# A wavelet convolution kernel with a similarity filter: norms kept as strips, six loads per unit instead of eleven, one store per band, another order of the residual's matmuls, and raw statistics one unit later

## The chip, the cores and the metric

The kernel runs on one core of a Trainium2 chip. The metric is device time in microseconds (us) of one launch. The kernel before took 2227.2, 2228.85 and 2239.03 us in three runs, median 2228.85 us.

## The reference

The input `x` is a batch of 8 images, 32 channels, 128 x 128, float32. Two layers follow one another, each of them on a group norm with 32 groups (here one channel each) and added to its input:

```
x = x + L0(gn(x))     # three Haar levels; at each a 5x5 convolution, 128 -> 128 channels, on the
                      # four stacked half-size bands; then the inverse transform, plus a bias
x = x + L1(gn(x))     # below, with the 25 patches (shifted images) of a pixel
    dot    = einsum('bchw,bckhw->bkhw', x, patches)
    sim    = dot / maximum(|x| * |patch|, 1e-8)
    weight = (sim + 1) * 0.5 * spatial_weight[k]
    out    = einsum('bckhw,bkhw->bchw', patches, weight)
```

## The kernel before

**Stages.** The program loops over images. In one pass it does the convolutions of image i and, in the same stretch, the similarity layer of image i - 1 (b in the code). The first pass has convolutions alone, the last the similarity layer alone, so there are eight image stages with a similarity layer. An image at half size has four quadrants of 32 channels, which fill the 128 partitions.

**Units.** The similarity layer of an image is cut into 8 units: four bands of rows, two halves each. For every unit (h or u in the code) ScalarE and VectorE make normalised vectors (`st_hl`, high and low fp16 part), values (`st_v`, the same) and norms (`st_n`). TensorE adds the squares over channels (`norm_piece`, two pieces per unit, into `stat_ps`), ScalarE keeps them and takes roots (`norms`), VectorE refines (`units_open`, `units_refine`, `units_close`, `value_lows`, `unit_lows`), ScalarE counts pixels whose norm is so small that the 1e-8 decides (`count_own`); only where this count is not zero does a guard path run. Each unit has 4 overlapping column groups (strips) of 10 columns; `st_hl` and `st_v` are kept as strips (4 x 18 x 10 = 720 elements), `st_n` as an image (18 x 34 = 612).

**The way through DRAM.** The layout must turn from "quadrant and channel in partitions" to "channel in partitions, quadrants along the row". `save_half` on SP's queue writes a unit's `st_hl`, `st_v` and `st_n` to DRAM in five transfers, `load_unit` reads them back in eleven: two for the keys, four for the queries, one for the values, four for the norm strips of 72 pieces with 10 elements each. SP's order within an image stage is save 0, load 0, save 1, load 1, save 2, and then for u = 0 to 7: the store of a finished band of rows (u = 2, 4, 6), save u + 3, load u + 2. A load of unit u waits until the save of the same unit has landed, and (from u = 2) until TensorE has used up unit u - 2, whose buffer it takes. Units have two buffers in `unit_mem`.

**Unit by unit.** After the level-2 and level-1 convolutions TensorE runs the 8 units. Each has 8 Gram products (`gram`), 30 matmuls of the level-0 convolution, the norm pieces of unit u + 3, the transposed values (`key_values`), the residual image (`residual`, 16 matmuls into 4 column groups) and four filter groups (`filter_group`), all woven together by the list `HOOKS`. VectorE turns every Gram product into weights (`weights`) and does its part of the convolution and the preparation of unit u + 3 between these. `unit_here` is TensorE's wait for a unit's loads.

**The other queue.** POOL's queue carries the raw image, in 8 chunks, once for statistics and once for use, through a ring of four slots; the small level-2 and level-1 images `d_z2` and `d_z1`; and `up`, their upsampled copies. ScalarE may write again over the buffer `z1` only when the save of `d_z1` has landed.

**Lines.** L381, L383 and L384 save a unit. L399 loads keys, L402 queries, L404 values, L409 norm strips. L416 stores a band. L454 and L483 are POOL's raw and `up` loads. L1339 is the Gram product, L1297 the norm piece, L1364 the residual, L1375 the filter.

Of the kernel before, what the change touches and what calls it, by code (L numbers as in the profile page):

```python
# [21 lines left out]
F32 = mybir.dt.float32  # L22
# [6 lines left out]
P = 128  # L29
C = 32  # L30
# [48 lines left out]
SAVES, LOADS = 80, 176  # L79
# [4 lines left out]
PAD_EDGE = P * (SH + SW - 1)  # L84
# [71 lines left out]
def build(nc, x, w0, w1, w2, bias, spatial, square, gather, tapmask, unpair, out):  # L156
    ctx = ExitStack()
    with ctx:
# [27 lines left out]
        st_n = sb("st_n", [P, 2, UN], F32)  # L186
# [59 lines left out]
        d_n = dram("d_n", [B, 2 * BANDS, Q, UN], F32)  # L246
# [113 lines left out]
        def _(sp):  # L360
# [16 lines left out]
            def save_half(b, h):  # L377
# [6 lines left out]
                sp.dma_start(d_n[b, h], st_n[0:P:C, h % 2, :]).then_inc(half_saved[h % 2], 16)  # L384

            def load_unit(b, u):
# [19 lines left out]
                norms = d_n[b, u].rearrange("(a q) (h w) -> a (q h) w", a=1, w=SW)  # L406
# [31 lines left out]
            sp.wait_ge(stored, START + 4 * 64 * B)  # L438
# [3 lines left out]
        def _(pool):  # L442
# [42 lines left out]
            def iteration(i, nxt, conv, ls):  # L485
                if conv:
# [10 lines left out]
                    raw_for_stats(i + 1, nxt, range(SLOTS, CHUNKS))  # L497
# [26 lines left out]
        def _(act):  # L524
# [44 lines left out]
            def result(b, u):  # L569
# [5 lines left out]
                if half == 0:  # L575
                    act.wait_ge(stored, START + 64 * (4 * b + r))
# [46 lines left out]
            def norms(b, h, p):  # L623
# [8 lines left out]
                copy(st_n[:, h % 2, p * PIECE:(p + 1) * PIECE], stat_ps[:, 0:PIECE]).then_inc(n2_kept, 1)  # L632
                if p == 1:
                    act.wait_ge(n2_kept, START + 16 * b + 2 * h + 2)
                    act.wait_ge(unit_low, START + 8 * b + h)
                    copy(st_b[:, :], st_a[:, :], func=ACT.Square).then_inc(root_squared, 1)
                    copy(in_strips(st_v[:, 0, h % 2, :]), strips(st_x2[:, h % 2, :, :].rearrange("p h w -> p (h w)"))).then_inc(v_high, 1)

            def count_own(b, h):
# [3 lines left out]
                nc.scalar.activation(st_hl[:, 1, h % 2, 0:UN], st_n[:, h % 2, :], ACT.Sign, bias=edge[:, :], scale=-1.0,  # L643
# [11 lines left out]
            def iteration(i, conv, ls):  # L655
# [45 lines left out]
                for j in range(CONV_TILES):  # L701
                    if conv and j == 2:
                        root(gn1, gn1_var, gn1_root, i + 1)
# [52 lines left out]
        def _(dve):  # L756
# [190 lines left out]
            def units_open(b, h):  # L947
# [7 lines left out]
                ch.link(dve, V.scalar_tensor_tensor(out=st_b[:, :], in0=st_b[:, :], scalar=-0.5, in1=st_n[:, h % 2, :],  # L955
                                                    op0=ALU.mult, op1=ALU.mult))

            def units_refine(h):
                sq = st_n[:, h % 2, :]
# [583 lines left out]
```

## Time and profile before

| | us |
|---|---|
| median of three runs | 2228.85 |
| the profiled execution | 2231.01 |
| its span in the trace | 2229.3 |
| TensorE matmul busy | 1737.3 |
| VectorE busy | 1363.9 |
| ScalarE busy | 742.9 |
| POOL busy | 430.6 |

### The profile page before, as it was taken

The page shows a single profiled execution, that of the slowest core. Times are in us where ns is not written, and L with a number is a line of the kernel's source. Part 1 is how long each engine was busy: PE and PEld are TensorE (multiplying, and loading weights), DVE is VectorE, ACT ScalarE, POOL GpSimd, SP SyncE. Part 2 cuts the span into 40 slices and gives each one's busy share as a digit, 9 for nine tenths or more (in the row PEclk, how much of TensorE's full clock was granted, in tenths as well). Part 3 has the DMA queues.
Part 4 walks back from the last instruction along what each step waited for, and adds up shares of the span by engine and source line. Part 5 has one row for each costly group of instructions (what it writes and reads, how often), then busy time and mean ns, then how long its engine had stood idle before and what let it go on. Part 6 is the DMA issues. An engine that isn't in the chain of part 4 may idle for free.

```text
span 2229.3 us, 53057 instructions
## 1 busy us (share of the span) xinstructions
PE 1737.3 (78%) x19007; PEld 988.9 (44%) x19007; DVE 1363.9 (61%) x1995; ACT 742.9 (33%) x1318; POOL 430.6 (19%) x760
## 2 busy tenths in 40 slices
PE   5776887978878787878778787878779787876576
PEld 3542344545444444535345344545345444443354
DVE  6427756756677456856577456755578465865453
ACT  2320243423333243423333243423333252423341
POOL 1343322012311123012310123012300224010000
PEclk7888897889989898989989898999989898987577
DMA  5243337552666337562656447552754447571555
GB/s 164 75 106 95 85 104 174 151 137 78 187 155 159 94 104 191 153 140 78 179 156 151 97 114 196 152 139 79 176 149 128 117 105 201 127 174 38 141 145 127
DMA packets 128073, 296.57 MB, mean 133 GB/s; under 512 B 44532, under 2 KB 77300, under 8 KB 127220
## 3 DMA queue, kind: packets, MB, share of 16 engines
q1 hardware_dynamic: 90864, 190.39, 33.5%
q0 software_dynamic: 36864, 101.47, 17.6%
q8 instruction: 230, 3.77, 0.8%
q14 instruction: 115, 0.94, 0.1%
HBM read 221.92 MB, written 69.83 MB: 131 GB/s over the span
## 4 chain that ended last, share of the span: by engine, by line
PE 41%; DMA 17%; DVE 15%; SPq 13%; issue 10%; ACT 2%; DVEq 1%; POOL 1%; ACTq 0%; POOLq 0%
PE conv L1274 11%; DMA unit_mem<-d_n 8%; DMA d_n<-st_n 8%; PE conv L1248 6%; PE gram L1339 5%; PE out_ps L1364 5%; PE out_ps L1375 3%; SPq L409 3%; PE conv L1233 3%; PE stat_ps L1297 3%; SPq L383 3%; SPq L402 2%; SPq L381 2%; PE vals_ps L1322 2%; PE conv L1484 2%
## 5 line engine op out<-in xcount | busy, mean ns | idle before, releaser
L1012 DVE SCALAR_TENSOR_TENSOR wgt<-gram,tapw 124x512 f32<-124x512 f32 x512 | 350.1, 685 | 476.9 <-PE gram L1339 441.2
L1274 PE MATMUL conv<-thl,wconv 128*128 128x496 f16 (+2 forms) x1920 | 535.5, 407 | 20.0 <-DVE xa L892 10.7
L454 POOL DMA_DIRECT2D ring<-in_x x576 | 334.1, 585 | 666.5 <-ACT xa L526 345.0
L1339 PE MATMUL gram<-unit_mem 128*60 128x128 f16 x4096 | 250.6, 247 | 210.1 <-DMA unit_mem<-d_n 137.9
L1339 PEld LDWEIGHTS gram<-unit_mem 128*60 128x60 f16 x4096 | 152.3, 113 | 420.0 <-issue 419.5
L1274 PEld LDWEIGHTS conv<-thl,wconv 128*128 128x128 f16 x1920 | 167.3, 103 | 215.3 <-issue 62.1
L1248 PE MATMUL conv<-thl,wconv 128*128 128x480 f16 (+7 forms) x1200 | 256.9, 368 | 0.0
L483 POOL DMA_DIRECT2D up<-d_z x128 | 68.5, 537 | 813.1 <-DVE xa L943 755.4
L1297 PE MATMUL stat_ps<-st_sq,sq_c 128*128 128x306 f32 x256 | 117.9, 549 | 125.5 <-DVE flag L993 40.4
L1375 PE MATMUL out_ps<-wgt,vals 124*32 124x128 f32 x4096 | 204.8, 296 | 0.8 <-DVE wgt L1012 0.4
L526 ACT ACTIVATE vals<-vals_ps 124x512 f32<-124x512 f32 x128 | 76.2, 596 | 341.3 <-PE vals_ps L1322 337.6
L526 ACT ACTIVATE thl<-tw 128x1024 f16<-128x1024 f32 x64 | 67.6, 1057 | 339.8 <-DVE tw L828 186.4
L1248 PEld LDWEIGHTS conv<-thl,wconv 128*128 128x128 f16 x1200 | 116.1, 98 | 123.4 <-issue 8.8
L1364 PE MATMUL out_ps<-x,sq_c 128*32 128x128 f32 x2048 | 169.0, 289 | 0.0
L1364 PEld LDWEIGHTS out_ps<-x,sq_c 128*32 128x32 f32 x2048 | 147.9, 115 | 19.9 <-issue 16.2
L526 ACT ACTIVATE st_a<-stat_ps,tiny 128x306 f32<-128x306 f32 x128 | 65.7, 514 | 218.4 <-DMA d_n<-st_n 112.3
L1375 PEld LDWEIGHTS out_ps<-wgt,vals 124*32 124x32 f32 x4096 | 124.3, 115 | 29.3 <-issue 6.4
L526 ACT ACTIVATE ostage<-out_ps,live 128x256 f32<-128x256 f32 x128 | 55.0, 486 | 205.2 <-PE out_ps L1375 205.2
L1297 PEld LDWEIGHTS stat_ps<-st_sq,sq_c 128*128 128x128 f32 x256 | 47.6, 223 | 151.6 <-issue 92.3
L955 DVE SCALAR_TENSOR_TENSOR st_b<-st_b,st_n 128x612 f32<-128x612 f32 x64 | 50.5, 789 | 104.5 <-ACT st_b L526 104.0
L1233 PE MATMUL conv<-xa,gat_c 128*128 128x512 f32 x128 | 79.0, 773 | 35.4 <-issue 19.1
L1322 PE MATMUL vals_ps<-unpair_c,unit_mem 64*60 64x32 f16 x4096 | 89.5, 183 | 1.7 <-issue 1.6
(137 smaller groups left out, 2110.8 us busy)
## 6 DMA issues: line engine op xcount, KB each, us to landing
unit_mem<-d_hl SPq DMA_DIRECT2D x128, 360.0 KB
unit_mem<-d_hl SPq DMA_DIRECT2D x256, 180.0 KB
ring<-in_x POOLq DMA_DIRECT2D x288, 128.0 KB, 3.4
ring<-in_x POOLq DMA_DIRECT2D x288, 127.0 KB, 3.7
d_hl<-st_hl SPq DMA_DIRECT2D x128, 180.0 KB
d_v<-st_v SPq DMA_DIRECT2D x128, 180.0 KB
unit_mem<-d_v SPq DMA_DIRECT2D x64, 360.0 KB
up<-d_z POOLq DMA_DIRECT2D x160, 128.0 KB, 4.9
```

Source lines behind the costliest of these rows:

```text
L454: pool.dma_start(dst, src).then_inc(raw_in[slot], 16)
L483: pool.dma_start(up[C * q:C * q + C, :].rearrange("c (b n) -> c b n", b=2), src).then_inc(up_in, 16)
L526: return nc.scalar.activation(dst, src, func, bias=bias, scale=scale)
L1012: V.scalar_tensor_tensor(out=dst, in0=g, scalar=SIM_SCALE ** 2, in1=tapw[:, :].unsqueeze(1).to_broadcast([KN, 2, 2 * QN]), op0=ALU.add, op ...
L1233: last = mm(dst, gat_c[:, q, :], src[:, 2 * r0 + q // 2:2 * r1:2, q % 2:2 * side:2], start=(q == 0), stop=(q == Q - 1))
L1248: last = mm(dst[:, a0 - r0:a1 - r0, b0:b1], wconv[:, level - 1, w, t, :], src[:, a0 + dy:a1 + dy, b0 + dx:b1 + dx], start=(n == 0), stop=( ...
L1274: last = mm(dst[:, :, b0:b1], wconv0[:, w, 2 * (p % ROWS4) + s, dx + 2, :], thl[:, p % 2, d, s, :, b0 + dx:b1 + dx] if p % ROWS4 != 1 else ...
L1297: mm(stat_ps[:, 0:PIECE], same_quadrant, st_sq[:, p * PIECE:(p + 1) * PIECE], start=True, stop=True)\
L1322: last = mm(vals_ps[row:row + KQ, C * n:C * n + C], values[s][0:2 * C, q, e, TH * KW * g:TH * KW * g + KQ], unpair_c[:, :], start=True, st ...
L1339: last = mm(bank[row:row + KQ, col:col + QN], key[:, q, e_at, TH * KW * g:TH * KW * g + KQ], tile[:, :, TH * g + 1:TH * g + 1 + TH, 1:1 + ...
L1364: last = mm(o[C * g:C * g + C, q, :].rearrange("p (h w) -> p h w", h=TH), ident[:, C * q:C * q + C], x1[:, row:row + TH, UW * half:UW * (h ...
L1375: last = mm(o[C * g:C * g + C, :, :, TW * e:TW * e + TW], vals[:, (e * BANDS + g) * 2 + c, :], wgt[:, e % 2, g, c * QN:(c + 1) * QN], star ...
```

## The change

Six edits.

- The norms are written as strips by VectorE (`st_s`, two buffers), and saved as strips, so that a unit's norm strips load as two contiguous rows. `st_n` has one buffer. The wait for the save before last moves from the copy of the norms to ScalarE's copy of the values and VectorE's write of the strips. Counting and the guard path follow the new layout and scale.
- Keys load in one transfer and queries in two. The source of each begins with a dimension of 2 and step 0.
- A band is stored in one transfer, whose DRAM side begins with the dimension of four groups.
- The residual's matmuls run over quadrants outside and column groups inside.
- VectorE's raw statistics of the next image move from ahead of and inside unit 0 to units 0 and 1, the group norm's steps after them by one unit.
- On POOL's queue the raw loads 4 to 7 for statistics come after the save of `d_z1` and its first `up` load, and `up` load 1 ahead of the raw loads for use.

The core of the diff (without constants of the count, and the lines that only pass a parameter on):

```diff
-SAVES, LOADS = 80, 176
+SAVES, LOADS, BAND_STORES = 80, 96, 16
@@ tensors
-        st_n = sb("st_n", [P, 2, UN], F32)
+        st_n, st_s = sb("st_n", [P, UN], F32), sb("st_s", [P, 2, FN], F32)
-        d_n = dram("d_n", [B, 2 * BANDS, Q, UN], F32)
+        d_n = dram("d_n", [B, 2 * BANDS, GROUPS, Q, SN], F32)
@@ SP: save_half
-                sp.dma_start(d_n[b, h], st_n[0:P:C, h % 2, :]).then_inc(half_saved[h % 2], 16)
+                sp.dma_start(d_n[b, h].rearrange("e q n -> q e n"), st_s[0:P:C, h % 2, :].rearrange("p (e n) -> p e n", e=GROUPS)).then_inc(half_saved[h % 2], 16)
@@ SP: load_unit
-                for j in range(2):
-                    sp.dma_start(keys[s][2 * C * j:2 * C * (j + 1)].rearrange("c q e n -> c (q e n)"),
-                                 d_hl[b, u].rearrange("l c q n -> (l c) (q n)")).then_inc(unit_in[s], 16)
-                for j, hl in enumerate((0, 0, 1, 1)):
-                    sp.dma_start(queries[s][C * j:C * j + C].rearrange("c q e n -> c (q e n)"),
-                                 d_hl[b, u, hl].rearrange("c q n -> c (q n)")).then_inc(unit_in[s], 16)
+                sp.dma_start(keys[s].rearrange("p q e n -> p (q e n)"),
+                             d_hl[b, u].rearrange("(a l) c q n -> a (l c) (q n)", a=1).to_broadcast([2, 2 * C, Q * FN])).then_inc(unit_in[s], 16)
+                for hl in range(2):
+                    sp.dma_start(queries[s][2 * C * hl:2 * C * (hl + 1)].rearrange("p q e n -> p (q e n)"),
+                                 d_hl[b, u, hl:hl + 1].rearrange("l c q n -> l c (q n)").to_broadcast([2, C, Q * FN])).then_inc(unit_in[s], 16)
...
-                for e in range(GROUPS):
-                    row = 64 + C * (e // 2)
-                    sp.dma_start(norm_strips[s][row:row + 1, e % 2].rearrange("a (n w) -> a n w", w=KW),
-                                 norms[:, :, TW * e:TW * e + KW]).then_inc(unit_in[s], 16)
+                for a in range(2):
+                    row = 64 + C * a
+                    sp.dma_start(norm_strips[s][row:row + 1].rearrange("p e n -> p (e n)"),
+                                 d_n[b, u, 2 * a:2 * a + 2].rearrange("(p e) q n -> p (e q n)", p=1)).then_inc(unit_in[s], 16)
@@ SP: store_band
-                for g in range(BANDS):
-                    row = 2 * (BH * r + TH * g)
-                    sp.dma_start(out[b, :, row:row + 2 * TH, :].rearrange("c h w -> c (h w)"),
-                                 ostage[C * g:C * g + C].rearrange("c h w -> c (h w)")).then_inc(stored, 16)
+                rows = out[b, :, 2 * BH * r:2 * BH * (r + 1), :].rearrange("c (g h) w -> g c (h w)", g=BANDS)
+                sp.dma_start(rows, ostage[:, :, :].rearrange("p h w -> p (h w)")).then_inc(stored, 16)
@@ POOL: iteration
-                    raw_for_stats(i + 1, nxt, range(SLOTS, CHUNKS))
                     pool.wait_ge(z1_done, 2 * i + 2)
...
                     load_up(i, 0)
+                    raw_for_stats(i + 1, nxt, range(SLOTS, CHUNKS))
+                    load_up(i, 1)
                     raw_for_split(i + 1, nxt, range(SLOTS))
-                    load_up(i, 1)
@@ ACT: norms
-                    act.wait_ge(half_saved[h % 2], START + SAVES * (4 * b + h // 2))
...
                     copy(st_b[:, :], st_a[:, :], func=ACT.Square).then_inc(root_squared, 1)
+                    act.wait_ge(half_saved[h % 2], START + SAVES * (4 * b + h // 2))
@@ DVE: units_refine
-                prep_chain.link(dve, V.scalar_tensor_tensor(out=sq, in0=sq, scalar=EPS_SIM ** -0.5, in1=st_a[:, :],
-                                                            op0=ALU.mult, op1=ALU.mult))
+                dve.wait_ge(half_saved[h % 2], START + SAVES * (4 * b + h // 2))
+                prep_chain.link(dve, V.tensor_tensor(in_strips(st_s[:, h % 2, :]), strips(st_n[:, :]), strips(st_a[:, :]), ALU.mult))
@@ DVE: iteration
-                    raw_stats(i + 1, 0)
-                    raw_stats(i + 1, 1)
                     level1_out(i, 0)
...
-                            if k < 4 and j == 0:
-                                raw_stats(i + 1, SLOTS + k)
+                            if k < 4 and j < 2:
+                                raw_stats(i + 1, SLOTS * j + k)
@@ PE: residual
-                for g in range(BANDS):
-                    row = BH * r + TH * g
-                    for q in range(Q):
+                for q in range(Q):
+                    for g in range(BANDS):
+                        row = BH * r + TH * g
```

SP's queue, first image stage: the end of save 0 and the whole of load 0, with the sizes of each transfer's destination. Before:

```order
L383 DMA d_v<-st_v 4x32x720 x2
L384 ISA
L384 DMA d_n<-st_n 4x612
L388 ISA
L396 ISA
L399 DMA unit_mem<-d_hl 64x2880 x2
L402 DMA unit_mem<-d_hl 32x2880 x4
L404 DMA unit_mem<-d_v 64x2880
L409 DMA unit_mem<-d_n 1x72x10
L409 ISA
```

The last transfer comes four times in all. The same place in the changed kernel:

```order
L383 DMA d_v<-st_v 4x32x720 x2
L384 ISA
L384 DMA d_n<-st_s 4x4x180
L388 ISA
L396 ISA
L398 DMA unit_mem<-d_hl 128x1x2880
L401 DMA unit_mem<-d_hl 64x1x2880 x2
L403 DMA unit_mem<-d_v 64x2880
L407 DMA unit_mem<-d_n 1x1440
L407 ISA
```

Eleven load instructions have become six, with the same bytes. Keys fill 128 partitions at once and queries 64 each; their sources, which the rows don't show, have the sizes 2 x 64 x 2880 and 2 x 32 x 2880.

POOL's queue in the pass of the first image, around the save of the level-1 image (`d_z<-sd`); `ring` is the raw image. Before:

```order
L454 DMA ring<-in_x 32x8x128
L454 DMA ring<-in_x 32x8x127
L499 DMA d_z<-sd 128x1024
L483 DMA up<-d_z 32x2x512 x4
L454 DMA ring<-in_x 32x8x128
L454 DMA ring<-in_x 32x8x127
```

And in the changed kernel:

```order
L485 DMA d_z<-z 128x256
L491 DMA up<-d_z 32x4x256 x4
L494 DMA d_z<-sd 128x1024
L479 DMA up<-d_z 32x2x512 x4
L450 DMA ring<-in_x 32x8x128
L450 DMA ring<-in_x 32x8x127
```

The 16 raw loads that stood ahead of the level-1 image's save now stand behind it and its first `up` load.

## Rows read from the trace of the kernel before

**Rows 1.** The page: span, engine totals, chain that ended last.
```profile
span 2229.3 us, 53057 instructions
...
PE 41%; DMA 17%; DVE 15%; SPq 13%; issue 10%; ACT 2%; DVEq 1%; POOL 1%; ACTq 0%; POOLq 0%
PE conv L1274 11%; DMA unit_mem<-d_n 8%; DMA d_n<-st_n 8%; PE conv L1248 6%; PE gram L1339 5%; PE out_ps L1364 5%; PE out_ps L1375 3%; SPq L409 3%; PE conv L1233 3%; PE stat_ps L1297 3%; SPq L383 3%; SPq L402 2%; SPq L381 2%; PE vals_ps L1322 2%; PE conv L1484 2%
```

**Rows 2.** SP's queue, third of eight image stages: start us, length us, issue.
```profile
807.11 1.50 SPq L381 DMA_DIRECT2D d_hl<-st_hl  x2
...
810.26 0.57 SPq L384 DMA_DIRECT2D d_n<-st_n  x1
818.24 1.23 SPq L399 DMA_DIRECT2D unit_mem<-d_hl  x2
...
821.59 0.47 SPq L404 DMA_DIRECT2D unit_mem<-d_v  x1
822.16 4.08 SPq L409 DMA_DIRECT2D unit_mem<-d_n  x4
...
841.99 1.22 SPq L399 DMA_DIRECT2D unit_mem<-d_hl  x2
...
970.35 1.16 SPq L399 DMA_DIRECT2D unit_mem<-d_hl  x2
```

**Rows 3.** TensorE, same image, units 6 and 7: start us, length us, idle before.
```profile
984.87 0.63 PE L1339 MATMUL gram<-unit_mem 128*60 128x128 f16 x8 [13.46 <-DMA unit_mem<-d_n]
...
1003.31 0.47 PE L1339 MATMUL gram<-unit_mem 128*60 128x128 f16 x8 [0.26 <-issue]
...
1019.80 0.64 PE L1375 MATMUL out_ps<-wgt,vals 124*32 124x128 f32 x16
```

**Rows 4.** Stretches of 1 us: engines busy, PEclk, DMA share, GB/s.
```profile
810.00:811.00 1.00, 1.00 (x6) 0.49 (x5) 0.97 (x2) 1.00 (x3) 0.00 (x0) 1.00 0.27 98
...
816.00:817.00 1.00, 1.00 (x5) 0.53 (x6) 0.00 (x0) 0.00 (x0) 0.00 (x0) 1.00 0.26 94
...
820.00:821.00 1.00, 1.00 (x7) 0.59 (x5) 0.00 (x0) 0.02 (x1) 0.00 (x0) 1.00 0.97 276
...
825.00:826.00 1.00, 1.00 (x6) 0.47 (x5) 0.97 (x3) 0.85 (x3) 0.00 (x0) 1.00 1.07 225
...
847.00:848.00 1.00, 1.00 (x28) 1.00 (x27) 0.60 (x1) 0.00 (x0) 0.00 (x0) 1.00 0.97 368
```

**Rows 5.** The view of the DMAs: queues' totals, transfers by size.
```profile
q0 software_dynamic: 36864, 101.47, 17.6%
q8 instruction: 230, 3.77, 0.8%
...
unit_mem<-d_hl SPq DMA_DIRECT2D x128, 360.0 KB
unit_mem<-d_hl SPq DMA_DIRECT2D x256, 180.0 KB
...
d_hl<-st_hl SPq DMA_DIRECT2D x128, 180.0 KB
...
unit_mem<-d_v SPq DMA_DIRECT2D x64, 360.0 KB
...
out<-ostage SPq DMA_DIRECT2D x128, 128.0 KB, 3.2
```

**Rows 6.** SP's queue, last image stage: first and last unit load.
```profile
2067.87 1.23 SPq L399 DMA_DIRECT2D unit_mem<-d_hl  x2
...
2197.33 1.49 SPq L399 DMA_DIRECT2D unit_mem<-d_hl  x2
```

**Rows 7.** TensorE: unit 1's second norm piece, residual and filter of unit 2.
```profile
871.10 1.39 PE L1297 MATMUL stat_ps<-st_sq,sq_c 128*128 128x306 f32 x2 [4.95 <-ACT st_n L526]
...
899.30 2.13 PE L1364 MATMUL out_ps<-x,sq_c 128*32 128x128 f32 x29
...
903.89 0.65 PE L1375 MATMUL out_ps<-wgt,vals 124*32 124x128 f32 x16
```

More of the change, by code:

```diff
@@ L628, in norms @@
                     act.wait_ge(unit_vec, START + 8 * b + h)
-                    act.wait_ge(half_saved[h % 2], START + SAVES * (4 * b + h // 2))
                 copy(st_a[:, p * PIECE:(p + 1) * PIECE], stat_ps[:, 0:PIECE], func=ACT.Abs_reciprocal_sqrt,
                      bias=tiny[:, :])
-                copy(st_n[:, h % 2, p * PIECE:(p + 1) * PIECE], stat_ps[:, 0:PIECE]).then_inc(n2_kept, 1)
+                copy(st_n[:, p * PIECE:(p + 1) * PIECE], stat_ps[:, 0:PIECE]).then_inc(n2_kept, 1)
                 if p == 1:
@@ L701, in iteration @@
                 for j in range(CONV_TILES):
-                    if conv and j == 2:
+                    if conv and j == 3:
                         root(gn1, gn1_var, gn1_root, i + 1)
@@ L954, in units_open, with units_refine @@
                 dve.wait_ge(root_squared, 8 * b + h + 1)
-                ch.link(dve, V.scalar_tensor_tensor(out=st_b[:, :], in0=st_b[:, :], scalar=-0.5, in1=st_n[:, h % 2, :],
+                ch.link(dve, V.scalar_tensor_tensor(out=st_b[:, :], in0=st_b[:, :], scalar=-0.5, in1=st_n[:, :],
                                                     op0=ALU.mult, op1=ALU.mult))
-            def units_refine(h):
-                sq = st_n[:, h % 2, :]
+            def units_refine(b, h):
                 prep_chain.link(dve, V.scalar_tensor_tensor(out=st_a[:, :], in0=st_b[:, :], scalar=1.5, in1=st_a[:, :],
                                                             op0=ALU.add, op1=ALU.mult))
-                prep_chain.link(dve, V.scalar_tensor_tensor(out=sq, in0=sq, scalar=EPS_SIM ** -0.5, in1=st_a[:, :],
-                                                            op0=ALU.mult, op1=ALU.mult))
+                dve.wait_ge(half_saved[h % 2], START + SAVES * (4 * b + h // 2))
+                prep_chain.link(dve, V.tensor_tensor(in_strips(st_s[:, h % 2, :]), strips(st_n[:, :]), strips(st_a[:, :]), ALU.mult))
             def image_of(h):
@@ L992, in set_flag @@
                 pads = PAD_EDGE if h // 2 in (0, BANDS - 1) else PAD_INNER
-                V.tensor_scalar(flag[:, h % FLAGS:h % FLAGS + 1], stat_ps[0:1, 0:1], 0.5, float(P * UN // 2 - pads), ALU.mult, ALU.add)\
+                V.tensor_scalar(flag[:, h % FLAGS:h % FLAGS + 1], stat_ps[0:1, 0:1], 0.5, float(P * FN // 2 - pads), ALU.mult, ALU.add)\
                     .then_inc(flag_done, 1)
@@ L1056, in iteration @@
                         units_open(b, h)
-                        units_refine(h)
+                        units_refine(b, h)
                         units_close(b, h)
@@ L1091, in iteration @@
                                 if k == 4:
-                                    units_refine(h)
+                                    units_refine(b, h)
                                 if k == 5:
@@ L1112, in iteration @@
                                 image_stats(i, 0, k - 3)
-                            if k < 4 and j == 0:
-                                raw_stats(i + 1, SLOTS + k)
-                            if k == 4 and j == 0:
+                            if k < 4 and j < 2:
+                                raw_stats(i + 1, SLOTS * j + k)
+                            if k == 4 and j == 1:
                                 gn_open(gn1, bn1, bn1_done, gn1_part, i + 1, CHUNKS)
-                            if k == 4 and j == 1:
+                            if k == 4 and j == 2:
                                 gn_mean(gn1, gn1_chain, gn1_part, gn1_mm, i + 1)
-                            if k == 6 and j == 1:
+                            if k == 6 and j == 2:
                                 gn_spread(gn1, gn1_mm, gn1_var, i + 1)
-                            if k == 3 and j == 2:
+                            if k == 3 and j == 3:
                                 gn_close(gn1, gn1_chain, gn1_root, gn1_done, i + 1, X_SCALE)
@@ L1455, in hook @@
                                 if k == 7:
-                                    count_short(b, j + AHEAD, i + 2 if conv_on and j == 1 else None)
+                                    count_short(b, j + AHEAD, i + 2 if conv_on and j == 2 else None)
                                 if k in (0, 2):
@@ L1460, in hook @@
                                 filter_group(b, j, 3)
-                        if conv_on and j == 1 and k in (4, 6):
+                        if conv_on and j == 2 and k in (4, 6):
                             if ls and k == 4:
-                                pe.wait_ge(n2_kept, START + 16 * b + 10)
+                                pe.wait_ge(n2_kept, START + 16 * b + 12)
                             gn_products(gn1, gn1_part, gn1_mm, i + 1, k // 5)
```

17 lines of the change are left out of this document (7 added, 10 removed).

## The prediction

> **What bounds the kernel now.** I read the page first: in the chain that ended last TensorE has 41%, DMA 17%, VectorE 15% and SP's queue 13%, and the two DMA lines in it are the last transfers of a unit's save and of its load [rows 1]. So the trip through DRAM is on the path beside TensorE. Then SP's queue, over one image stage: save 0 takes from 807.1 to its landing just before 818.24, where load 0 goes out; issuing load 0 takes until 826.24; load 1 can't go before 841.99, when save 1 has landed [rows 2]. Then TensorE's own rows: it stands still for 13.46 us ahead of unit 6, whose norm strips land late, and then does unit 6 in 18.4 us and unit 7 by 1020.44 [rows 3]. Last the stretches of 1 us, which say how many DMA engines worked.
>
> **What the DMA share says.** While save 0 alone is moving, the share stands flat at 0.26 to 0.27, with 94 to 98 GB/s, for seven microseconds, although four transfers of 180 KB are queued [rows 2, 4, 5]. The share means 0.26 x 16 = 4.2 engines, and the DRAM side of a save begins with a dimension of 4. The loads, whose sides begin with 64 or 32 on both ends, bring the share to 0.97 to 1.07 [rows 4]. So a transfer is spread over as many engines as the first dimension of both its sides allows, four for the saves; and since four such transfers together also stay at 0.26, each takes the same four. One engine then moves 94/4 to 98/4, some 23.8 GB/s; over the seven stretches from 810 to 817 the mean is 22.6, which I take for stores. A loading engine at best moved 368/0.97/16 = 23.7 GB/s [rows 4]; 23.7 for loads.
>
> The new keys and queries have a source that begins with a dimension of 2. By the same reading they run on two engines, the same two each time, and the band store (first dimension 4) on four. The rest of this sum follows from that.
>
> The Trainium skill says it outright, in "DMA: Bandwidth & Descriptors", section "Why a DMA increments its semaphore by 16 and not by 1": the engine count is the largest number up to 16 that divides the slowest non-size-1 dimension of both sides, and from SP it is always the lowest-numbered engines. Its "Rules for kernel authors" warn that a leading zero-stride broadcast of c copies confines the whole DMA to at most c engines. The saves' 0.26 agrees for c = 4; no run yet shows it for a step of zero. By a plain count of transfers (six issues for eleven, same bytes) the change would be a gain instead, which is rival A.
>
> **The sum, for one image stage, from the issue of load 0 to the end of unit 7.** Before, 818.24 to 1020.44 = 202.2 us [rows 2, 3]. After, the two busiest engines set it:
> - keys 737,280 bytes and queries the same (360 KB x 2 and 180 KB x 4, as before) [rows 5]: 1,474,560 / 2 / 23.7 = 31.1 us; values 368,640 / 16 / 23.7 = 1.0. A load is 32.1 us, eight are 257.
> - saves 1 to 7: 737,280 / 4 / 22.6 = 8.2 us each on the same engines, 57.
> - band stores 0 and 1 (524,288 / 4 / 22.6 = 5.8), 12; store 2 stands behind load 7.
> - POOL's transfers in the stretch: 12 raw chunks of 0.52 MB, four `up` loads of 0.52 and the save of `d_z1`, 8.9 MB over 16 engines. POOL's queue moved 101.47 MB in 17.6% of 16 engines' span, 16.2 GB/s an engine [rows 5]: 34 us. Instruction fetches, 0.8% of the span [rows 5]: 2.
> - breaks: load 0's first byte 2, save 1's landing before load 1 goes 2, landing of load 7 to TensorE 1.5.
> - unit 7 itself: 18.4, as unit 6 after its stop, at the lower clock at first [rows 3].
>
> 257 + 57 + 12 + 34 + 2 + 5.5 + 18.4 = 386 us, so +184 for each of seven images.
>
> Is the queue never idle in between? The other work of a unit takes 18 to 24 us, less than 32.1 + 8.2 = 40.3. Load u + 2 goes out when unit u is done, while load u + 1 still moves for some 15 us; save u + 3 stands ahead of it, and save u + 2, for whose landing it waits, is ahead of load u + 1 (from u = 1). Only save 1 to load 1 has a break, counted above.
>
> The last image has no convolution and no raw loads. Before, 2067.87 to 2229.3 = 161.4 [rows 1, 6]. After: 257 + 57 + 12 + 2 + 5.5 = 334, then the last unit and its results (18), and the last store, 5.8 and 2 to land: 360. That is +198.
>
> Together 2231.0 + 7 x 184 + 198 = 3717, say 3715 us. The sum starts from the profiled execution, 2231.0, which is 2.2 above the median 2228.85: less than anything here.
>
> **The other edits,** all beside a TensorE that will wait some 20 us in each unit, so I cost them at nothing:
> - Norm strips: 288 pieces of 40 bytes per unit become two rows of 5,760 bytes, and the issue, 4.08 us now, becomes about 1 [rows 2]. Free again, it would be worth part of the 13.46 us of rows 3. If an engine takes a row alone it needs 0.25 us.
> - The strips' write on VectorE has 720 elements for 612, and so has the count on ScalarE: a sixth more elements in steps of under a microsecond.
> - The waits moved: the norm piece waited 4.95 us for ScalarE, held by save 2, in unit 1 [rows 7]. Now `units_refine` and the copy of the values wait for it. Save 2 stands behind load 1, lands some 10 us after unit 1 starts, which is when VectorE comes to the wait; queued behind are `units_close`, the weights from product 5 on, and so TensorE's filter groups. A few microseconds at most, and load 2 is on the rings meanwhile.
> - The residual: 32 records in 2.1 us; the filter, which goes round the column groups, does 16 in 0.65 [rows 7]. By that rate 1.3 us, 0.8 less per unit; were TensorE the bound, 51 us over 64 units. Hidden, it is nought.
> - Raw statistics and POOL's order: the same bytes, some of them later. They share the two engines whenever they come, and the sum has them. Their users, the fills of the next image from unit 5 on, come several units later.
> Bounds of these together: a gain of 20 if they shorten the way to load 0, a loss of 40 for breaks at units 1 and 2.
>
> **Rivals.**
> A. The zero step is not a dimension that counts, and keys and queries fill 16 engines. Then the stops go: some 12 of the 13.46 us at unit 6, 4.95 at unit 1, 6 of the residual, 2 to 4 of the issue before unit 0: about 26 us for each of eight images, 2231 - 208 = 2023. For it: nothing here has a step of zero in front. Against: the saves' count of engines follows the sizes alone. 0.07.
> B. Two engines, but another pair for each transfer, three side by side: keys land after 368,640 / 23.7 = 15.6 us, which a unit of 20 us nearly covers. Then about 2200. Against: the four transfers of a save never exceed 0.27 [rows 4]. 0.03.
> C. Two engines at the slow rate, 225 / 1.07 / 16 = 13.1 GB/s, that loads had around 825 [rows 4]: a load then takes 56 + 1 us, +25 each, over 64 units 1600 more, 5300. Against: that rate is one of 16 engines at once, and four alone had 22.6. 0.04.
>
> The side on which I could be wrong in sign is A: one mechanism, decided by whether a leading step of 0 limits the engines. It tips where keys and queries together take less than the 20 us of a unit, at four engines or more.
>
> **Chances and range.** The sum 0.86, A 0.07, B 0.03, C 0.04. Within the sum: a loading engine at 27 GB/s for want of company would take 3.9 us off each load, 3715 - 250 = 3465, and POOL's 34 us half outside the two engines' busy time 120 more, about 3350; loads at the mean rate of stores with breaks of 5 us per unit would add 100 + 320, 4130. Range 3330 to 4150, which leaves out a fifth with A, B and C. A measurement of this kernel can tell about 0.5%, 11 us, from no change. Slower: the sum and C, 0.90. Faster 0.09 (A, most of B), within 0.5% 0.01.
>
> **What would show it.** Right: stretches in the unit stage with a DMA share near 0.125 and 45 to 50 GB/s; load to load about 45 to 48 us on SP's queue in units 2 to 7; TensorE waiting some 20 to 25 us for `unit_mem` ahead of nearly every Gram product 0, and its clock at 1.2 GHz after each; DMA with over half of the chain; residuals 0.8 us shorter with no effect. Wrong: a share near 1 while keys load (A), 0.25 to 0.4 with a load done in 16 us (B), or two engines with less than 30 GB/s together (C).

## The result, and the profile after

The changed kernel took 3600.25 us in the median of four runs (3599.77 to 3604.61); the kernel before, beside it on the same chip, 2233.94 us (2227.2 to 2246.69). The ratio is 1.611, with a 95% interval of 1.603 to 1.619. The forecast was 3715 us with a range of 3330 to 4150, so the time lies in the range, 115 us below the forecast.

The page after: span, engines, queues, the chain that ended last by engine and by line, and two groups (busy and mean ns, then the idle time before them). SPq is SP's queue. It answers to [rows 1, 5].

```profile
span 3596.8 us, 52065 instructions
...
PE 1690.8 (47%) x19007; PEld 918.4 (26%) x19007; DVE 1377.7 (38%) x1995; ACT 754.4 (21%) x1318; POOL 429.4 (12%) x760
...
q1 hardware_dynamic: 62704, 190.46, 15.8%
q0 software_dynamic: 36864, 101.47, 11.0%
...
SPq 57%; DMA 17%; PE 15%; DVE 5%; issue 4%; ACT 1%; POOL 0%; DVEq 0%; ACTq 0%; POOLq 0%
SPq L401 18%; SPq L403 13%; DMA unit_mem<-d_n 11%; SPq L381 10%; SPq L383 9%; SPq L407 5%; DMA d_n<-st_s 4%; PE conv L1240 3%; PE conv L1266 3%; PE conv L1225 2%; SPq L384 2%; PE gram L1331 1%; SPq L398 1%; PE conv L1476 1%; PE out_ps L1367 1%
...
L1331 PE MATMUL gram<-unit_mem 128*60 128x128 f16 x4096 | 262.8, 256 | 1696.4 <-DMA unit_mem<-d_n 1675.4
...
L1356 PE MATMUL out_ps<-x,sq_c 128*32 128x128 f32 x2048 | 74.3, 289 | 0.0
```

The engines did the same work as before within a few per cent (TensorE 1690.8 us busy after 1737.3), and SP's queue moved 190.46 MB for 190.39. What grew is one wait: TensorE stood 1675.4 us for `unit_mem` ahead of the Gram products, where it was 137.9 us before (64 stops, one for every unit, of 26.2 us on the mean). The difference, 1537.5 us, is more than the whole loss of 1367.5 us between the spans. SP's queue now stands for 57% of the chain, and its issues of queries (L401), values (L403) and saves (L381, L383) lead the list of lines. SP moved its 190.46 MB in 15.8% of 16 engines' span, 20.9 GB/s for a busy engine; the same sum before, with 33.5% of 2229.3 us, gives 15.9. The engines that worked were not slow, there were few of them.

SP's queue in the third image stage after (start us, length us, issue), answering to [rows 2]:

```profile
1152.47 0.62 SPq L398 DMA_DIRECT2D unit_mem<-d_hl  x1
1153.19 5.64 SPq L401 DMA_DIRECT2D unit_mem<-d_hl  x2
1158.94 6.81 SPq L403 DMA_DIRECT2D unit_mem<-d_v  x1
1165.85 1.40 SPq L407 DMA_DIRECT2D unit_mem<-d_n  x2
1167.49 9.82 SPq L381 DMA_DIRECT2D d_hl<-st_hl  x2
1177.42 11.42 SPq L383 DMA_DIRECT2D d_v<-st_v  x2
1189.03 1.27 SPq L384 DMA_DIRECT2D d_n<-st_s  x1
1199.27 0.59 SPq L398 DMA_DIRECT2D unit_mem<-d_hl  x1
```

The first transfer of load 1 goes out 46.8 us after that of load 0 (23.8 before). The gaps after it are 48.9, 51.1, 46.0, 38.4, 43.7 and 27.7 us, against 29.6, 22.8, 23.3, 21.3, 21.8 and 9.5 before. The same rows show something new. The values' issue, 0.47 us before, takes 6.81, and the pair of L381 9.82 for 1.50. SP stands in the issue itself while the transfers ahead are still being moved.

Stretches of 1 us while load 0 is moving (engines busy, PEclk, DMA share, GB/s), answering to [rows 4]:

```profile
1158.00:1159.00 1.00, 1.00 (x6) 0.48 (x5) 0.85 (x2) 0.00 (x0) 0.00 (x0) 1.00 0.11 46
1161.00:1162.00 1.00, 1.00 (x7) 0.40 (x5) 0.88 (x3) 0.97 (x3) 0.00 (x0) 1.00 0.12 52
1167.00:1168.00 1.00, 0.98 (x7) 0.20 (x4) 0.00 (x0) 0.00 (x0) 0.00 (x0) 1.00 1.01 288
1190.00:1191.00 1.00, 0.17 (x4) 0.17 (x6) 0.00 (x0) 0.00 (x0) 0.00 (x0) 0.50 0.26 81
```

A share of 0.11 to 0.14 is two of 16 engines: keys and queries. At 1167 the values, a transfer that begins with 64, bring it to 1.01 for one microsecond. At 1190 save 1 moves alone at 0.26, four engines, as before. The mean over the ten stretches from 1156 to 1166 is 54.4 GB/s.

TensorE in the same image stage (the bracket is the idle time before), answering to [rows 3, 7]: units 0, 1, 2 and 7, the residual, and the last filter matmuls of unit 7.

```profile
1190.84 0.64 PE L1331 MATMUL gram<-unit_mem 128*60 128x128 f16 x8 [22.86 <-DMA unit_mem<-d_n]
1239.60 0.64 PE L1331 MATMUL gram<-unit_mem 128*60 128x128 f16 x8 [29.23 <-DMA unit_mem<-d_n]
1249.29 1.08 PE L1356 MATMUL out_ps<-x,sq_c 128*32 128x128 f32 x32
1298.89 0.64 PE L1331 MATMUL gram<-unit_mem 128*60 128x128 f16 x8 [39.55 <-DMA unit_mem<-d_n]
1509.28 0.63 PE L1331 MATMUL gram<-unit_mem 128*60 128x128 f16 x8 [16.72 <-DMA unit_mem<-d_n]
1526.09 0.65 PE L1367 MATMUL out_ps<-wgt,vals 124*32 124x128 f32 x16
```

All eight units wait, 16.72 to 39.55 us each; before, the longest stop of the stage was the 13.46 us ahead of unit 6. From 1152.47 to 1526.7 the stage takes 374 us, where the forecast had 386.

### The profile page after: what moved, and what is told of

Read it like the earlier page. It is cut to its first block, busy times and chain, and to the rows that moved or that the text cites. A ratio compares the mean times of both kernels' runs of the same rounds, so it can differ in the third digit from the quotient of the medians.

```text
span 3596.8 us, 52065 instructions
## 1 busy us (share of the span) xinstructions
PE 1690.8 (47%) x19007; PEld 918.4 (26%) x19007; DVE 1377.7 (38%) x1995; ACT 754.4 (21%) x1318; POOL 429.4 (12%) x760
## 3 DMA queue, kind: packets, MB, share of 16 engines
q1 hardware_dynamic: 62704, 190.46, 15.8%
## 4 chain that ended last, share of the span: by engine, by line
SPq 57%; DMA 17%; PE 15%; DVE 5%; issue 4%; ACT 1%; POOL 0%; DVEq 0%; ACTq 0%; POOLq 0%
SPq L401 18%; SPq L403 13%; DMA unit_mem<-d_n 11%; SPq L381 10%; SPq L383 9%; SPq L407 5%; DMA d_n<-st_s 4%; PE conv L1240 3%; PE conv L1266 3%; PE conv L1225 2%; SPq L384 2%; PE gram L1331 1%; SPq L398 1%; PE conv L1476 1%; PE out_ps L1367 1%
## 5 line engine op out<-in xcount | busy, mean ns | idle before, releaser
L1331 PE MATMUL gram<-unit_mem 128*60 128x128 f16 x4096 | 262.8, 256 | 1696.4 <-DMA unit_mem<-d_n 1675.4
L1331 PEld LDWEIGHTS gram<-unit_mem 128*60 128x60 f16 x4096 | 160.8, 119 | 1918.5 <-issue 1918.1
L1266 PE MATMUL conv<-thl,wconv 128*128 128x496 f16 (+2 forms) x1920 | 558.2, 421 | 14.6 <-DVE xa L902 9.9
L1367 PE MATMUL out_ps<-wgt,vals 124*32 124x128 f32 x4096 | 180.8, 299 | 0.9 <-DVE wgt L1008 0.9
L1289 PE MATMUL stat_ps<-st_sq,sq_c 128*128 128x306 f32 x256 | 129.9, 599 | 42.6 <-ACT st_sq L522 34.8
L1367 PEld LDWEIGHTS out_ps<-wgt,vals 124*32 124x32 f32 x4096 | 111.9, 118 | 30.3 <-issue 9.3
L1225 PE MATMUL conv<-xa,gat_c 128*128 128x512 f32 x128 | 78.5, 770 | 35.4 <-issue 20.1
L1314 PEld LDWEIGHTS vals_ps<-unpair_c,unit_mem 64*60 64x60 f16 x4096 | 80.0, 115 | 30.3 <-issue 30.2
L878 DVE TENSOR_TENSOR thl<-tw,thl 128x1024 f16<-128x1024 f32 x64 | 78.0, 1219 | 10.1 <-ACT thl L522 10.1
L1356 PE MATMUL out_ps<-x,sq_c 128*32 128x128 f32 x2048 | 74.3, 289 | 0.0
```

The costliest lines, as they stand in the source:

```text
L1266: last = mm(dst[:, :, b0:b1], wconv0[:, w, 2 * (p % ROWS4) + s, dx + 2, :], thl[:, p % 2, d, s, :, b0 + dx:b1 + dx] if p % ROWS4 != 1 else ...
L1331: last = mm(bank[row:row + KQ, col:col + QN], key[:, q, e_at, TH * KW * g:TH * KW * g + KQ], tile[:, :, TH * g + 1:TH * g + 1 + TH, 1:1 + ...
L1367: last = mm(o[C * g:C * g + C, :, :, TW * e:TW * e + TW], vals[:, (e * BANDS + g) * 2 + c, :], wgt[:, e % 2, g, c * QN:(c + 1) * QN], star ...
```

## The experiments

Each kernel is the changed one or the one before with the edit named. "4-way store" is the kernel before's band store in four transfers. Every ratio is against the kernel before on the same chip.

| kernel | keys, queries | saves, store | us, median | ratio (95%) |
|---|---|---|---|---|
| the change | 1 + 2 transfers | as changed | 3600.25 | 1.611 (1.603 to 1.619) |
| 1 old loads | 2 + 4 | as changed | 2147.17 | 0.959 (0.954 to 0.963) |
| 2 broadcast only, in before | 1 + 2 | as before | 3547.67 | 1.586 (1.578 to 1.594) |
| 3 keys only | 1 + 4 | as changed | 2829.92 | 1.263 (1.257 to 1.269) |
| 4 old loads, 4-way store | 2 + 4 | store as before | 2139.45 | 0.954 (0.949 to 0.958) |
| 4 again | 2 + 4 | store as before | 2138.50 | 0.959 (0.951 to 0.966) |
| 5 quadrant saves | 2 + 4 | saves in 8 of 32 partitions | 2033.78 | 0.911 (0.904 to 0.918) |
| 6 old residual | 2 + 4 | as 4 | 2180.97 | 0.977 (0.969 to 0.985) |
| 7 old raw order | 2 + 4 | as 4 | 2153.37 | 0.967 (0.958 to 0.976) |
| 8 change, quadrant saves | 1 + 2 | saves as 5 | 3273.72 | 1.461 (1.458 to 1.465) |
| 9 padded keys | 2 of 64 partitions, + 4 | as changed | 2889.34 | 1.292 (1.288 to 1.295) |
| 10 without strips | as before | as before | 2207.91 | 0.985 (0.981 to 0.990) |
| 11 strips only | as before | as before | 2197.14 | 0.981 (0.976 to 0.985) |

**1 and 2: the cause, taken out and put in alone.** In kernel 1 the change has the old transfers of keys and queries:

```diff
-                sp.dma_start(keys[s]..., d_hl[b, u]....to_broadcast([2, 2 * C, Q * FN]))...
-                for hl in range(2):
-                    sp.dma_start(queries[s][2 * C * hl:2 * C * (hl + 1)]..., d_hl[b, u, hl:hl + 1]....to_broadcast([2, C, Q * FN]))...
+                for j in range(2):
+                    sp.dma_start(keys[s][2 * C * j:2 * C * (j + 1)]..., d_hl[b, u]...)...
+                for j, hl in enumerate((0, 0, 1, 1)):
+                    sp.dma_start(queries[s][C * j:C * j + C]..., d_hl[b, u, hl]...)...
```

Three dots in the code stand for what is left out of a line; the two transfers of keys fill 64 partitions each, the four of queries 32 each.

Kernel 2 is the kernel before with this diff the other way round, and nothing else of the change.

> The changed kernel with the keys and queries loaded as before, in two and four transfers without a leading step of zero; all other edits stay. Theory (a source that begins with a dimension of 2 confines a transfer to two DMA engines, and this alone costs the time): the time falls below the kernel before, to 2000 to 2150 us, and a load brings the DMA share to about 1. Rival (another edit of the change makes the loss, such as the moved waits or POOL's new order): it stays above 2500 us.

> The kernel before with the keys and queries alone loaded as in the change. Theory: nearly all of the loss comes with this one edit, 3500 to 3750 us, with stretches at a DMA share of 0.12 to 0.14 while keys and queries load. The changed kernel took 3600; its other edits are hidden behind the loads. Rival (the loss needs another edit): under 2500 us.

Measured 2147.17 and 3547.67 us. The three transfers alone make the loss; without them the change is a gain of 4%. Kernel 1's load 0 in stretches of 1 us, in the third image stage:

```profile
795.00:796.00 1.00, 1.00 (x3) 0.29 (x2) 0.00 (x0) 0.00 (x0) 0.00 (x0) 0.50 0.79 242
796.00:797.00 1.00, 1.00 (x4) 0.41 (x3) 0.00 (x0) 0.00 (x0) 0.00 (x0) 0.55 0.99 236
797.00:798.00 1.00, 1.00 (x7) 0.43 (x5) 0.00 (x0) 0.00 (x0) 0.00 (x0) 1.00 1.05 242
```

The same bytes fill 16 engines again. Rival A's step (the zero step does not count) is thereby excluded for keys and queries together; whether the two or the step of zero is what counts is asked by kernel 9.

Kernel 2's issues, same image stage, show an issue that stands for 23 us, close to the longest of that run (23.29):

```profile
1141.21 0.64 SPq L398 DMA_DIRECT2D unit_mem<-d_hl  x1
1141.95 4.44 SPq L401 DMA_DIRECT2D unit_mem<-d_hl  x2
1146.50 0.52 SPq L403 DMA_DIRECT2D unit_mem<-d_v  x1
1147.12 23.12 SPq L408 DMA_DIRECT2D unit_mem<-d_n  x4
```

**3: half of it.** The change, with the queries in four transfers as before, so that only the keys (737,280 bytes) run on two engines.

> The changed kernel with the queries loaded as before, and only the keys in one transfer with the leading step of zero. Theory: two engines carry 368,640 bytes each for the keys at 27.2 GB/s, the rate that the changed kernel's trace shows for them, 13.6 us, with 1.9 for queries, 1 for values, 8.2 for a save and some 5 for stores and POOL: about 29 us a unit instead of 46, near a unit's own 20 to 25 us, so most of the loss goes: 2300 to 2600 us. Rival (the cost is in reading a row twice, or goes with the bytes so loaded, wherever they move): half of the loss stays, about 2850 us.

Measured 2829.92 us: outside what my theory said, and at the rival's number. My argument was that 13.6 us on two engines would mostly hide beside a unit of 20. SP's queue, third image stage:

```profile
966.17 0.61 SPq L398 DMA_DIRECT2D unit_mem<-d_hl  x1
...
970.62 7.95 SPq L381 DMA_DIRECT2D d_hl<-st_hl  x2
978.67 11.04 SPq L383 DMA_DIRECT2D d_v<-st_v  x2
989.90 1.43 SPq L384 DMA_DIRECT2D d_n<-st_s  x1
1001.97 0.59 SPq L398 DMA_DIRECT2D unit_mem<-d_hl  x1
```

Load 1 goes out 35.8 us after load 0, in kernel 1 it is 19.0. Later loads follow after 36.1, 39.1, 35.4, 26.1 and 31.8 us (27.6, 25.4, 23.1, 20.7, 23.0 in kernel 1). The wait for a save and the load stand in one row: load 0, save 1 behind it on the same engines, then load 1. And these engines had little room even before: 8.2 us of a save, some 8 of a load (1,843,200 bytes at kernel 1's 242 GB/s), and some 4 of POOL's transfers (34 a stage over eight units), some 20 us of a unit of 20 to 25. So what is added to them adds to the unit. The period of an image goes from 239.6 us (kernel 1) to 326.1 (kernel 3) to 422.7 (the change), +86.5 and +96.6, that is 10.8 and 12.1 us for each of eight loads, and each step puts the same 368,640 bytes on each of the two engines, 13.6 us at the 27.2 GB/s measured above, in place of the 46,080 that each of 16 carried: 322,560 more, 11.9 us. Nearly the whole added transfer time arrives. The first half is not hidden.

**4: the band store.** Kernel 1 with the store in four transfers of 32 rows, as before:

```diff
-                rows = out[b, :, 2 * BH * r:2 * BH * (r + 1), :].rearrange("c (g h) w -> g c (h w)", g=BANDS)
-                sp.dma_start(rows, ...)...
+                for g in range(BANDS):
+                    row = 2 * (BH * r + TH * g)
+                    sp.dma_start(out[b, :, row:row + 2 * TH, :]..., ostage[C * g:C * g + C]...)...
```

> As the kernel with all loads as before, and the band store too in four transfers over 16 engines. Theory: a store on four engines takes 5.8 us of their time once in two units, beside units of 20 us, and is hidden while loads fill all 16 engines: within 1% of the kernel with the old loads alone, if anything up to 30 us less. Rival (engines 0 to 3 are the bound also with the old loads): 50 us less or more.

> The kernel with loads and store as before and the rest of the change once more, on the chip of the three others, for their differences: 2139 us within 0.5%.

Measured 2139.45 and, in another set of runs, 2138.50 us. The intervals overlap with kernel 1's: with the old loads the store on four engines costs nothing that can be told.

**5 and 8: the saves on more engines.** Kernel 5 is kernel 4 with each save by quadrants:

```diff
-                for hl in range(2):
-                    sp.dma_start(d_hl[b, h, hl].rearrange("c q n -> q c n"), st_hl[:, hl, h % 2, :])
+                for q in range(Q):
+                    sp.dma_start(d_hl[b, h, :, :, q, :].rearrange("l c n -> c l n"), st_hl[C * q:C * q + C, :, h % 2, :])
```

and the same for `st_v`. The first dimension of both sides is now 32 instead of 4. Kernel 8 is the changed kernel with this edit alone.

> The kernel with loads and store as before and the rest of the change (2139 us), and a unit's vectors and values saved in eight transfers, one for each quadrant, whose first dimension is 32 on both sides, for four whose DRAM side begins with 4. Theory (the first dimension sets the engines, and the saves' four are near their limit also with the old loads): the DMA share goes from 0.26 to near 1 during saves, a save needs some 3 us of all engines for 8.2 of four, SP issues four more, and the time falls by 5 to 12 us an image, to 2040 to 2100 us. Rival (the saves are hidden, or SP's issue takes back what they free): 2139 us, or more.

> The changed kernel (3600 us) with its vectors and values saved in eight transfers over 16 engines for four over four. Theory (the two busiest engines' time sets the image stage, and the saves are one term of it): 184,320 bytes of a save, 8.2 us on each of these engines, become 46,080 bytes, 2 us; 6 us less for each of seven saves of eight images, 340 us less: 3220 to 3320 us. Rival (only the loads' own two engines and the wait for them count, saves run beside them): within 50 us of 3600.

Measured 2033.78 us for kernel 5, the fastest of all, 9% below the kernel before and 6 us below the range expected, and 3273.72 for kernel 8, 327 us below the change and inside its range. Kernel 5's save 0 and the start of load 0, and stretches in that save:

```profile
756.77 1.83 SPq L381 DMA_DIRECT2D d_hl<-st_hl  x4
758.70 1.79 SPq L383 DMA_DIRECT2D d_v<-st_v  x4
760.68 0.69 SPq L384 DMA_DIRECT2D d_n<-st_s  x1
762.85 1.20 SPq L399 DMA_DIRECT2D unit_mem<-d_hl  x2
```

```profile
758.00:759.00 1.00, 1.00 (x6) 0.45 (x5) 0.00 (x0) 0.97 (x3) 0.00 (x0) 1.00 0.77 182
759.00:760.00 1.00, 1.00 (x6) 0.49 (x5) 0.59 (x1) 1.00 (x3) 0.00 (x0) 1.00 0.81 187
```

The save moves at 182 to 187 GB/s, at a share of 0.77 to 0.81 (expected was near 1), for the 94 to 98 of [rows 4], and load 0 leaves 6.1 us after the save's first issue (11.1 before). Four more issues per save cost less than this gives. TensorE's wait for `unit_mem` over the whole program falls from 158.7 us (kernel 4 again) to 53.2, and TensorE has half of the chain:

```profile
PE 50%; DVE 21%; issue 13%; SPq 4%; DMA 4%; ACT 4%; DVEq 2%; POOL 1%; ACTq 0%; POOLq 0%
...
L1334 PE MATMUL gram<-unit_mem 128*60 128x128 f16 x4096 | 251.5, 247 | 122.3 <-DMA unit_mem<-d_n 53.2
```

**9: two, or the step of zero?** Kernel 1, with the DRAM tensor `d_hl` made one row longer per half, so that high and low part no longer lie end to end. The two key transfers are those of before, with the same bytes into 64 partitions, but their source stays 2 x 32 x 2880 with a real step between the two.

```diff
-        d_hl = dram("d_hl", [B, 2 * BANDS, 2, C, Q, FN], F16)
+        d_hl = dram("d_hl", [B, 2 * BANDS, 2, C + 1, Q, FN], F16)[:, :, :, 0:C]
-                                 d_hl[b, u].rearrange("l c q n -> (l c) (q n)")
+                                 d_hl[b, u].rearrange("l c q n -> l c (q n)")
```

> The changed kernel with queries loaded as before and keys in two transfers of 64 partitions, from a DRAM tensor with one unused row between the high and the low parts, so that each source has the sizes 2 x 32 x 2880 with a step that is not zero. Theory (the number 2 in front confines, whatever its step): the keys again lie on two engines with 368,640 bytes each, and the time is that of the kernel with the keys alone in one transfer with a step of zero, 2830 us within 2%. Rival (the step of zero is what confines or slows): 2147 us, as with all loads as before.

Measured 2889.34 us, 2.1% above the number and so just outside the 2% allowed, where the rival had the time of kernel 1. Why it takes 59 us more than kernel 3 (ratios 1.292 and 1.263, intervals apart) stays open. While the keys move:

```profile
983.00:984.00 1.00, 1.00 (x8) 0.47 (x7) 0.14 (x1) 0.00 (x0) 0.00 (x0) 1.00 0.13 46
984.00:985.00 1.00, 1.00 (x7) 0.54 (x6) 0.00 (x0) 0.00 (x0) 0.00 (x0) 1.00 0.12 46
```

Two engines again. The leading 2 confines a transfer with a step of zero and with the one other step tried. By the rule of the Trainium skill that the prediction named (the page "DMA: Bandwidth & Descriptors"), both cases come out at two engines, and both runs agree.

**6, 7, 10 and 11: what the other edits are worth when they aren't hidden.** Kernel 6 is kernel 4 with the residual's old loop order, kernel 7 is kernel 4 with the raw statistics and POOL's order as before:

```diff
-                for q in range(Q):
-                    for g in range(BANDS):
+                for g in range(BANDS):
+                    for q in range(Q):
```

```diff
+                    raw_for_stats(i + 1, nxt, range(SLOTS, CHUNKS))
                     pool.wait_ge(z1_done, 2 * i + 2)
...
                     load_up(i, 0)
-                    raw_for_stats(i + 1, nxt, range(SLOTS, CHUNKS))
-                    load_up(i, 1)
                     raw_for_split(i + 1, nxt, range(SLOTS))
+                    load_up(i, 1)
```

and `raw_stats` of VectorE back to units 0 and earlier. Kernel 10 is the kernel before with the change's residual order and raw order, and without its strips; kernel 11 is the kernel before with the strips alone.

> The same kernel with loads and store as before (2139 us), with the residual's matmuls in the old order. Theory (the new order lets four column groups work together, and TensorE sets the pace in most units): 0.8 us for each of 64 units come back, 25 to 55 us more, 2165 to 2195 us. Rival (units wait for VectorE or DMA anyway): within 10 us.

> The same kernel with loads and store as before (2139 us), with the raw statistics, the group norm's steps and POOL's queue in the old order. Theory (raw loads beside the first saves and VectorE's waits for them in unit 0 cost some microseconds an image): 10 to 40 us more. Rival (they only move the traffic): within 10 us.

> Before, with two of the change's edits only: the residual's order and the raw statistics one unit later with POOL's order. Norms, loads, saves and store are before's. Theory (the edits add): the residual gave 42 us and the raw order some 15 where the other edits were present, so about 2234 - 57 = 2177, within 2155 to 2195; the rest of the 95 us is then the norm strips'. Rival (the strips gave nothing by themselves, and what these two edits save is more): 2135 to 2150.

> Before, with the norm strips only (two norm rows per unit instead of four transfers of 40-byte pieces, one transfer fewer and the moved wait); residual, raw order, keys, queries, saves and store as before. Theory: SP issues each load some 3 us sooner, which every unit whose load lands late gives back; about 2234 - 40 = 2194, within 2175 to 2215. Rival (the stop ahead of unit 6 is set by the transfers' bytes, not by the issue of the norm pieces): 2225 to 2240.

Measured 2180.97, 2153.37, 2207.91 and 2197.14 us. The residual gives 42 us (kernel 6 against 4 again). The raw order gives 15 (kernel 7 against 4 again) with intervals that overlap, so it isn't shown. The strips give 43 us by themselves (1.9%). Residual and raw order together give 32 us by themselves, which is less than the theory said (57) and less than its range. A part of the rest turned into a wait, as the waits for `unit_mem` over the whole program show: kernels 10 and 11, then kernel 6's residual.

```profile
PE gram L1335 <- DMA unit_mem<-d_n: 161.4, 37, 12.6
```

```profile
PE gram L1338 <- DMA unit_mem<-d_n: 110.1, 21, 8.5
```

```profile
L1359 PE MATMUL out_ps<-x,sq_c 128*32 128x128 f32 x2048 | 166.6, 285 | 0.3 <-issue 0.3
```

The columns of the first two are total us, times, and the longest. The kernel before has 137.9 us there. Shortening TensorE's units without helping the loads (kernel 10) adds 23.5 us of waiting; the strips (kernel 11) take 27.8 away. Beside it stands a lower clock. Kernel 10's runs had a granted clock of 0.855 to 0.865, the runs of the kernel before on the same chip 0.870 to 0.887, and TensorE's matmuls other than the residual's are busy 1618.4 us in its profile (1695.5 - 77.1) for 1568.3 (1737.3 - 169.0) before. So the edits seem to need each other: 43 and 32 apart, about 95 together. The ratios of 0.981 and 0.985 multiply to 0.966, kernel 4 has 0.954 and, again, 0.959 with an interval that ends at 0.966. How much of this is the wait and how much the clock isn't shown. In the residual's group 2048 matmul records are busy 166.6 us in kernel 6 and 75.6 in kernel 4 again, with about the same mean length (285 and 292 ns). So in the new order, where neighbours go to different column groups, more of them run side by side.

## Why the prediction was right, and where its numbers were off

**Which engines a transfer gets.** This was the step that carried the sign, and it held: 0.11 to 0.14 for keys and queries, by kernels 1 and 2 the whole of the loss, by kernel 9 with a step other than zero too. Rivals A, B and C fall with it. A was the zero step not counted; B expected a share of 0.25 to 0.4; C expected under 30 GB/s from two engines, and there were 54.4.

**The rate of a lone loading engine, a term that was mis-sized.** The sum had 23.7 GB/s, the best that 16 engines at once had shown; measured are 54.4 / 2 = 27.2. Keys and queries take 27.1 us, not 31.1: 4 us a load, 32 a stage, 256 over eight stages. The text had this case as its lower bound (27 GB/s, 3465 us), and with it the sum falls 135 us below the measured time.

**The shared engines under mixed traffic, the term that was too small.** With the rate put right, a stage would be 386 - 32 = 354 us, and it was 374. The last image stage, where POOL moves nothing, shows most of the difference. Its load 0 goes out at 3254.12, and units 0 and 7 begin with these rows:

```profile
3288.13 0.64 PE L1331 MATMUL gram<-unit_mem 128*60 128x128 f16 x8 [24.93 <-DMA unit_mem<-d_n]
3571.04 1.06 PE L1331 MATMUL gram<-unit_mem 128*60 128x128 f16 x16 [19.55 <-DMA unit_mem<-d_n]
```

Unit 0 begins 34.0 us after the issue, where 27.1 + 1.0 + 3.5 = 31.6 would do. In the 282.9 us up to unit 7 lie seven loads, seven saves and two band stores, by the rates 7 x (27.1 + 1.0 + 8.2) + 12 = 266. Together some 19 us are missing; the sum had 4 of them, 2 for a break ahead of load 1 and 2 for fetches. Stretches of 1 us there:

```profile
3296.00:3297.00 1.00, 1.00 (x28) 0.80 (x18) 0.05 (x1) 0.82 (x1) 0.00 (x0) 0.50 0.00 0
3342.00:3343.00 1.00, 0.31 (x8) 0.12 (x4) 0.97 (x2) 0.55 (x1) 0.00 (x0) 1.00 0.14 46
3350.00:3351.00 1.00, 0.00 (x0) 0.00 (x0) 0.00 (x0) 0.00 (x0) 0.00 (x0) 0.50 0.12 52
```

The engines stand still only ahead of load 1, for some 3 us from 3295. From 3299 to 3551 no stretch has a share below 0.11, the share of two engines, so there is no other break: the shared engines weren't idle, they were slower. Each of the two moved 6.87 MB in the 282.9 us, 24.3 GB/s, between the 22.6 of saves alone and the 27.2 of keys and queries alone. At 3342, when load 2 has just begun, the share is already that of two engines, with 46 GB/s. Why the rate drops there is open.

POOL's term nearly held. In the third stage, with POOL's transfers, unit 0 begins 38.4 us after the issue and unit 7 318.4 us later, together 39.9 us more than in the last, where 34 was forecast; unit 7 then took 17.4 us for 18.4. The last image took 342.7 us (forecast 360).

The two errors have opposite signs, some 250 us too much and some 155 too little. That the total came out 3% below the forecast is in part luck; the range held without it. Two readings of the prediction were off. The seven stretches of save 0 move 79 to 98 GB/s, not 94 to 98 (their mean of 22.6 GB/s an engine is right). And the stops ahead of the units were 26.2 us on the mean, for 20 to 25.

**Who shows it in the chain.** The forecast had DMA with over half of the chain; it has 17%, and SP's queue 57%. The trip through the engines is what was meant, but SP stands inside its issues, and the chain stops there. The trace before had signs of it that I did not read: six pairs of L383 that lasted 6.14 to 10.93 us where most take 1.4.

**The other edits.** "Hidden" holds inside the change, with one reservation. Kernel 2, which lacks them all, is 53 us faster than the change (ratios 1.586 and 1.611, intervals apart), so together they cost there, more than the bound of 40 given for breaks. The sum's own store term, 5.8 us twice a stage on the busy four engines, is over 90 us and would be enough. The traces point to it: in the third stage the two gaps between loads that hold a band store are 46.0 and 43.7 us in the change and 42.0 and 39.5 in kernel 2. This was not run by itself. With the old loads (kernel 4) they are worth about 95 us, and the issue of the strips fell from 4.08 us [rows 2] to 0.81.

**The point at which it tips, which was wrong.** The text held that the change stops costing where keys and queries take less than the 20 us of a unit, "at four engines or more", and B's 2200 rests on the same thought (15.6 us nearly covered). Kernel 3 refutes it: 13.6 us on the two engines cost 683 us over the program. The engines to be counted are those that saves and loads have in common, with everything that stands on them in a unit; a unit's length less that is the room, and it was near nothing. Rival A's 2023 us was too low too: with full loads the kernel takes 2147, and TensorE's wait for `unit_mem`, which A took to be nearly gone, is 159.9 us in it. It comes to 2034 only when the saves too are spread, which A did not reckon with.

## What to carry to other kernels

Read the DMA share beside the sizes of both ends of a transfer: a share that stays flat at 2/16 or 4/16 while transfers queue says that a small leading dimension confines them. Split such a transfer by partitions instead of merging it; eight saves for four gave 105 us here, three loads for six cost 1453. Add up what the engines that all these transfers share have to do per unit before calling anything on them hidden.

## What the runs showed of the hardware

- A transfer whose DRAM side begins with 2 or 4 held the DMA share at 0.11 to 0.14 or 0.26 to 0.27, whatever was queued behind it on SP's queue; with 32 or 64 in front on both sides the share went to 0.77 and more.
- The two engines that loaded alone moved 27.2 GB/s each on the mean, four that saved alone 22.6 (19.8 to 24.5). With all sixteen at work it went either way: 14.4 (242 / 1.05 / 16) for the same keys and queries in kernel 1, 14.4 to 14.8 in kernel 5's saves (182 / 0.77, 187 / 0.81, over 16), but 23.7 in the best stretch of [rows 4]. Against the 54.4 GB/s of two engines that is 4.4 to 6.8 times as much for the loads.
- A pair or four of issues on SP's queue stood for up to 10.93 us before (L383), 19.81 in the change (L401) and 23.29 in kernel 2 (L408), while few engines carried all. What is behind them in SP's order goes out late even where most of its own engines are idle: the values in the change, issued 6.81 us long beside a share of 0.11 to 0.14, need 16 engines for about one microsecond.
- TensorE's granted clock fell to 0.50, the level of 1.2 GHz, in the stop ahead of unit 0 (TensorE has no work from 1168 on) and stayed there until 1199, with unit 0 already running since 1190.84; over the run it was 0.722 for the 0.885 of before. Its busy time on the Gram products rose only from 250.6 to 262.8 us, so the slower clock was not where the time went.
- With the residual's order over four column groups, the 32 records of its 16 fp32 matmuls take 1.08 us in a row; in the old order 29 of them take 2.13 [rows 7].
